# Routing inside the attention: the second stage of a transformer program is dissolved into the gaps of the first

## The reference, cut to what matters

```python
x = x + attention(layernorm(x)) @ Wo.T            # per head: softmax(q k^T * scale) v
h = layernorm(x)
logits = h @ gate_w.T                             # 14 experts
probs = softmax(logits)
top2_p, top2_i = top_k(probs, 2)
w = top2_p / max(top2_p.sum(-1), 1e-10)
x = x + clip(h + w0 * expert[top2_i[:, 0]](h) + w1 * expert[top2_i[:, 1]](h), -100, 100)
```

## Time and profile before

| | us |
|---|---|
| median of 3 runs | 2218.16 |
| lowest and highest | 2213.41, 2222.66 |
| the profiled execution | 2228.09 |
| its span, first to last instruction | 2226.4 |
| TensorE busy | 1696.7 (76%) |
| VectorE busy | 1467.5 (66%) |
| ScalarE busy | 1210.6 (54%) |
| GpSimd busy | 1360.6 (61%) |

### The profile page before, as it was taken

How to read it: one execution, slowest core, us unless ns; L and a number is a source line. 1 busy time by engine, 2 the same in 40 slices (tenths; PEclk the granted TensorE clock), 3 DMA queues, 4 the chain that set the end, 5 groups by cost and what they waited for, 6 DMA issues and landing times. The chain is left out here.

```text
span 2226.4 us, 59455 instructions
## 1 busy us (share of the span) xinstructions
PE 1696.7 (76%) x18769; PEld 1117.8 (50%) x18769; DVE 1467.5 (66%) x3940; ACT 1210.6 (54%) x2321; POOL 1360.6 (61%) x1087
## 2 busy tenths in 40 slices
PE   7978999999999999975442699377777766100997
PEld 3424656565566666645342588344444443000897
DVE  5756888888888888836444444178888887620453
ACT  4626888888888888854332355224444444021343
POOL 0005878787878887845446233488888883155465
PEclk9978999999999999985655799689999898555999
DMA  4753222222222222212221333400000000132332
GB/s 153 247 171 119 60 71 62 70 63 70 64 68 66 67 67 65 71 59 78 72 87 58 104 127 123 151 22 20 19 19 19 19 19 1 43 111 80 99 102 62
DMA packets 158123, 169.71 MB, mean 76 GB/s; under 512 B 39522, under 2 KB 124393, under 8 KB 157961
## 3 DMA queue, kind: packets, MB, share of 16 engines
q1 hardware_dynamic: 143128, 137.02, 20.1%
q0 software_dynamic: 13824, 29.43, 4.2%
q10 hardware_dynamic: 1008, 0.92, 0.1%
HBM read 93.57 MB, written 73.97 MB: 75 GB/s over the span
## 5 line engine op out<-in xcount | busy, mean ns | idle before, releaser
L769 DVE TENSOR_REDUCE halfmax<-p_m 128x1 f32<-128x512 f32 x1024 | 644.3, 681 | 125.8 <-PE p_m L638 123.1
L756 ACT ACTIVATE probs<-p_s,ESCALE 128x512 f32<-128x512 f32 x1024 | 643.9, 685 | 27.4 <-PE p_s L668 10.5
L638 PE MATMUL p_m<-ka,qa 96*32 96x512 f16 x4096 | 518.8, 390 | 12.8 <-DMA vh<-v 12.0
L668 PE MATMUL p_s<-qa,ka 98*32 98x512 f16 x4096 | 503.6, 383 | 8.8 <-DMA qa<-max_lo 6.4
L591 POOL TENSOR_TENSOR sum_p<-sum_p,probs 128x1024 f32<-128x1024 f32 x192 | 456.1, 2375 | 11.0
L675 PE MATMUL p_o<-probs,vh 128*32 128x256 f32 x4096 | 401.1, 380 | 0.3 <-ACT probs L756 0.3
L591 POOL TENSOR_TENSOR sum_p<-probs 128x1024 f32<-128x1024 f32 x64 | 152.2, 2378 | 165.8 <-ACT probs L756 165.8
L638 PEld LDWEIGHTS p_m<-ka,qa 96*32 96x32 f16 x4096 | 180.0, 97 | 125.0 <-DVE halfmax L769 19.4
L668 PEld LDWEIGHTS p_s<-qa,ka 98*32 98x32 f16 x4096 | 178.6, 96 | 122.1 <-ACT probs L756 12.4
L1652 PE MATMUL ln_p_cum<-ln_kv,c_tri 128*128 128x512 f32 (+1 forms) x384 | 166.5, 577 | 88.6 <-POOL ln_kv L1596 88.6
L1309 ACT ACTIVATE e_h<-e_p_h,e_w 128x256 f32<-128x256 f32 x316 | 126.1, 473 | 158.8 <-PE e_p_h L1288 84.8
(11 more groups left out here) (299 smaller groups left out, 2797.4 us busy)
## 6 DMA issues: line engine op xcount, KB each, us to landing
e_xb<-xs SPq DMA_DIRECT2D x40, 257.0 KB
e_xb<-xs SPq DMA_DIRECT2D x78, 128.0 KB, 2.0
ys<-e_y SPq DMA_DIRECT2D x78, 128.0 KB, 1.9
v<-pj_v SPq DMA_DIRECT2D x8, 1024.0 KB, 5.0
qa<-q SPq DMA_DIRECT2D x64, 128.0 KB, 2.7
ka<-k SPq DMA_DIRECT2D x64, 128.0 KB, 2.7
vh<-v SPq DMA_DIRECT2D x64, 128.0 KB, 2.2
o<-ot SPq DMA_DIRECT2D x64, 128.0 KB
```

Source lines behind the costliest of these rows:

```text
L638: mm = nc.tensor.matmul(max_bank(s, n)[j * DH0:(j + 1) * DH0, :], qa[s][0:KA, (n // 2) * P + j * DH0:(n // 2) * P + (j + 1) * DH0], ka[s][ ...
L668: mm = nc.tensor.matmul(score_bank(s, k, h)[j * DH0:(j + 1) * DH0, :], ka[s][:, cols], qa[s][:, q], start=True, stop=True, tile_position=( ...
L756: nc.scalar.activation(probs[k][:, h * HALF:(h + 1) * HALF], score_bank(s, k, h)[:, :], ACT.Exp, scale=ESCALE[:, 0:1]).then_inc(probs_d, 1)
L769: nc.vector.reduce_max(halfmax[s % 2][:, n // 2, n % 2:n % 2 + 1], max_bank(s, n)[:, :], AX.X).then_inc(max_read, 1)
```

## The change

`route2` is gone. Its work goes by whole sequences (8 tiles of 128 tokens) into `attend`, in "gaps": gap u is the place in TensorE's text around the denominators of unit u, and the place in VectorE's text behind the fourth maxima half, where the maxima are split. A sequence takes fifteen gaps from gap 12 + 8b on: 0 and 1 project, 1 and 2 add and take moments, 3 scales, 4 and 5 normalise and turn, 5 and 6 logits, 7 exponentials and the best two, 8 their indices, 11 counting and ranks, 12 places, 13 gates, and from 14 on GpSimd issues two scatters in each unit. Several sequences are under way at once. What belongs to gaps past 63 is done after the last unit, in the same block.

With it come: one PSUM bank for routing (`p_r`), taken from the maxima, which keep two of three; `TURN` 4 instead of 5, so that the maxima are turned just ahead of the denominators; the loops over units written out on all engines; the normalised rows kept in DRAM (`xn0`) instead of SBUF and read back to XN at the start of `e0`; zero rows written early in the attention; gate weights loaded before the experts' weights.

```diff
-TURN = 5
+TURN = 4
-MAX_BANKS = tuple(i % 3 for i in range(SLOTS * RING))
+MAX_BANKS = tuple(i % 2 for i in range(SLOTS * RING))
...
-        p_m = [ctx.enter_context(nc.psum_tensor(f"p_m{i}", [P, HALF], F32)) for i in range(3)]
+        p_m = [ctx.enter_context(nc.psum_tensor(f"p_m{i}", [P, HALF], F32)) for i in range(2)]
...
+        ST, NX, FIRST = KT, 3, 12
+        p_r = ctx.enter_context(nc.psum_tensor("p_r", [P, HALF], F32))
...
+        def sequence(gap, piece):
+            b, rest = divmod(gap - FIRST - piece, H0)
+            return b if rest == 0 and 0 <= b < B else None
...
         def _(sp):
...
+            load(SLOTS)
+            sp.wait_ge(zeros_d, 1)
+            zero_surplus(sp, xs, lambda n: zeros[:, :, :], E0, surplus_of(2, E0), surplus_out)
+            for u in range(UNITS):
+                if u + 2 < UNITS:
+                    rows_of_maxima(u + 2)
+                if u >= 1:
+                    spread_inverses(u - 1)
+                outputs_of = sequence(u, -1)
+                if outputs_of is not None:
+                    load_outputs(outputs_of)
+                if u >= 3:
+                    store(u - 3)
+                rows_of = sequence(u, 6)
+                if rows_of is not None:
+                    keep_rows(rows_of)
...
         def _(pool):
...
+            def scatter(h, half):
+                b = next((m for m in range(B) if 0 <= h - FIRST - 14 - m * H0 < H0), None)
+                if b is None:
+                    return
+                n = 2 * (h - FIRST - 14 - b * H0) + half
+                i, t, k = n // 8, n // 2 % G, n % 2
+                apart(pool, slot_d, b + 1, passed)
+                pool.indirect_dma_start(xs[:, :], bass.IndirectOffsetOnAxis(ap=slot[b % NX][:, n:n + 1], axis=0),
+                                        xn[b % NX][i][:, t, :], None).then_inc(rows_out[b % NX], 16)
...
+                    if n == 1 and u >= 3:
+                        normalise(u - 3)
+                    if n >= 2:
+                        scatter(u, n - 2)
...
         def _(pe):
...
+            def ranks(b):
+                pe.wait_ge(shift_d, 2 * b + 2)
+                if b + 1 < B - 1:
+                    pe.wait_ge(x_d, 2 * b + 4)
+                pe.wait_ge(hot_d, b + 1)
+                pe.wait_ge(seen_d, (b + 1) * ST)
+                nc.tensor.matmul(pos_ps, c["stri"][:, :], both[:, :, :], start=True, stop=False)
+                nc.tensor.matmul(pos_ps, c["ones"][:, :], seen[:, 0:ST, :], start=False, stop=True).then_inc(pos_d, 1)
...
             for u in range(UNITS):
-                rest_of_head(pe, u // SLOTS, u % SLOTS)
+                for k in range(2, KT):
+                    key_tile(u, k)
+                if u < LAST:
+                    for k in range(2):
+                        key_tile(u + 1, k)
+                if u + 2 < UNITS:
+                    max_turn(u + 2)
+                in_front(u)
+                denominators(u)
+                behind(u)
+            turn(B - 2, 0)
+            logits(B - 2, 0)
+            turn(B - 2, 1)
+            logits(B - 2, 1)
+            ranks(B - 2)
+            for i in range(2):
+                attention(B - 1, i)
+            for i in range(2):
+                turn(B - 1, i)
+                logits(B - 1, i)
+            ranks(B - 1)
...
         def _(act):
...
+                    if k == 4:
+                        b = sequence(u, 4)
+                        if b is not None:
+                            roots(b)
+                        if u:
+                            keep_outputs(u - 1)
...
         def _(dve):
...
+            def count_tiles(b):
+                dve.wait_ge(hot_d, b + 1)
+                from_first(dve, now_d, b)
+                from_first(dve, pos_d, b)
+                nc.vector.tensor_copy(seen[:, 0, :], seen[:, ST, :]).then_inc(seen_d, 1)
+                for t in range(ST - 1):
+                    dve.wait_ge(seen_d, b * ST + t + 1)
+                    nc.vector.tensor_tensor(seen[:, t + 1, :], seen[:, t, :], both[:, t, :], ALU.add).then_inc(seen_d, 1)
...
+            def segment(u):
+                if u + 1 < UNITS:
+                    row_maxima(u + 1)
+                for n in range(SCORES):
+                    if n == TURN:
+                        if u + 1 < UNITS:
+                            split_maxima(u + 1)
+                        if u >= 2:
+                            invert(u - 2)
+                        route(u - 1)
+                    if u + 2 < UNITS:
+                        half_max(u + 2, n)
...
-def route2(nc, c, X, XN, GATE, SLOT, tabs, o0, xs, wo, wg, oT):
...
+                for n in range(B):
+                    rows = slice(n * T, (n + 1) * T)
+                    sp.dma_start(kept[0][:, rows], kept[1][:, rows]).then_inc(kept_in, 16)
                 turned(sp, 0, 0, 0)
                 load(sp, AHEAD, 0, 1)
```

More of the change, by code:

```diff
@@ new lines, in attend @@
+        xT = sb("r_xT", [P, GT])
+        top, total, prob = sb("r_top", [P, G]), sb("r_total", [P, ST]), sb("r_prob", [P, ST, E0])
+        best, at = sb("r_best", [P, ST, 8]), sb("r_at", [P, ST, 8], U32)
+        atf, slotf = sb("r_atf", [P, ST, 2]), sb("r_slotf", [P, ST, 2])
+        hot, both = sb("r_hot", [P, ST, 2, E0]), sb("r_both", [P, ST, E0])
+        seen = sb("r_seen", [P, ST + 1, E0])
+        now, start = sb("r_now", [P, E0]), sb("r_start", [P, E0])
+        place, placed = sb("r_place", [P, ST, E0]), sb("r_placed", [P, ST, 2, E0])
@@ new lines, in denominators, with key_tile @@
+            def denominators(u):
+                pe.wait_ge(sum_p_d, SP0 + (u + 1) * len(POOL_SUMS))
+                spread(u, 1, c["ones"][:, 0:DH0], sum_p[u % 2], False, False)
+                for k in range(len(POOL_SUMS) + 1, KT):
+                    last = spread(u, 1, c["ones"][:, 0:DH0], probs[k], False, k == KT - 1)
+                last.then_inc(den_d, 1)
+            def key_tile(u, k):
+                nxt = (u, k + 2) if k + 2 < KT else (u + 1, k + 2 - KT)
+                for h in range(2):
+                    if nxt[0] < UNITS:
+                        score(*nxt, h)
+                    if u + 2 < UNITS:
+                        max_half(u + 2, 2 * k + h)
+                values(u, k)
@@ new lines, in attention @@
+            def attention(b, i):
+                pe.wait_ge(oT_in[i], (b + 1) * 32)
+                if i:
+                    pe.wait_ge(x_d, 2 * b + 1)
+                else:
+                    from_first(pe, shift_d, 2 * b)
+                if b == B - 1:
+                    pe.wait_ge(pos_read, B - 1)
+                for t in range(G):
+                    for cc in range(2):
+                        mm = nc.tensor.matmul(y_ps[:, t, :], oT[i][:, cc, t * P:(t + 1) * P], wo[:, cc, :],
+                                              start=(cc == 0), stop=(cc == 1))
+                mm.then_inc(y_d, 1)
@@ new lines, in turn, with logits @@
+            def turn(b, i):
+                pe.wait_ge(xn_d, 2 * b + i + 1)
+                if i:
+                    pe.wait_ge(shift_d, 2 * b + 1)
+                else:
+                    pe.wait_ge(x_d, 2 * b + 2)
+                    from_first(pe, pos_read, b)
+                for t in range(G):
+                    mm = nc.tensor.transpose(p_r[:, t * P:(t + 1) * P], xn[b % NX][i][:, t, :], c["ident"][:, :])
+                mm.then_inc(pxT_d, 1)
+            def logits(b, i):
+                pe.wait_ge(xT_d, 2 * b + i + 1)
+                for t in range(G):
+                    mm = nc.tensor.matmul(gate_ps[:, t, :], xT[:, t * P:(t + 1) * P], wg[:, :], start=True, stop=True)
+                mm.then_inc(gate_d, 1)
@@ new lines, in behind @@
+            def behind(gap):
+                b = sequence(gap, 0)
+                if b == 0:
+                    pe.wait_ge(weights_in, (E0 + 4) * 16)
+                if b is not None:
+                    attention(b, 0)
+                b = sequence(gap, 1)
+                if b is not None:
+                    attention(b, 1)
+                b = sequence(gap, 4)
+                if b is not None:
+                    turn(b, 0)
+                b = sequence(gap, 5)
+                if b is not None:
+                    turn(b, 1)
+                b = sequence(gap, 11)
+                if b is not None:
+                    ranks(b)
@@ L785, in invert @@
-        def invert(dve, r, s):
-            u = r * SLOTS + s
-            dve.wait_ge(few_in, ONE + (u + 1) * 16)
-            nc.vector.reciprocal(few[s % 2][:, :], few[s % 2][:, :]).then_inc(inv_d, 1)
+                    behind_tile(u, k)
+            for b in range(B - 2, B):
+                roots(b)
+                for i in range(2):
+                    for t in range(G):
+                        normalise(b, i, t)
+                for i in range(2):
+                    copy_turned(b, i)
+                exponentials(b)
@@ L825, in _ @@
+            invert(LAST - 1)
+            end = LAST % 2
```

939 lines of the change are left out of this document (403 added, 536 removed).

## The result

| | before | changed |
|---|---|---|
| median of the runs | 2215.8 us (4 runs, 2212.7 to 2222.7) | 2237.0 us (4 runs, 2233.2 to 2254.1) |
| ratio, with 95% interval | | 1.0102 [1.0054, 1.0150] |
| profiled execution | 2228.1 us | 2234.0 us |

The change made the kernel slower, by 1.0% on this chip. The forecast was 2192 us, 1% faster. Case B of the rivals had put 2239.

The account below looks back on a forecast made before the run. TensorE was taken to bound the attention (738.68 of 740 us busy), while routing hid nothing. -176 + 49 + 57 + 13 + 15 + 11 + 5 = -26 from 2228.1 gave 2202, less 9.9 for the median 2192 us; range 2125 to 2250.

Parts of the forecast that it names:

- Case B: Rival, attention: GpSimd's additions also hold up VectorE's operations of one SBUF input; VectorE's term 104, time 2239 us; chance 0.18.
- stage removed, with its tail: Routing between attention and experts: 262 us removed, a tail of 86 (78 to 105) left; saves 176 us.
- matmuls of TensorE: Attention: projections 25, turns 8, logits 13, ranks 3 added on full TensorE; together 49 us, nothing hides it.
- banks and turn: Attention: two banks for the maxima instead of three cost 15 us (0 to 38); the turn's new place nothing.
- start: Start of attention: first maxima bound by VectorE 3 us, zero DMAs ahead of unit 2's maxima rows 8; together 11.
- pauses of VectorE and ScalarE: Gaps of the attention: VectorE 57 us (31 for pauses, 26 for the counting chain), ScalarE 13 for normalising and table loads.
- experts and later: Start of the experts: normalised rows read back in eight DMAs, TensorE may wait; 5 us (0 to 12).
- One is much worse: Gap with the counting: eight dependent two-SBUF-input additions may each wait for GpSimd's; 5.2 us times five sequences, 26.
- 2.1 us each, 0.7 more than is free: Attention: VectorE's routing work over seven gaps per sequence; 44 such pauses cost 31 us.
- I take nothing: Attention: 76 of 128 scatters on GpSimd, 2.5 of 2.2 us spare per unit, within its slack; cost 0.
- Turning the maxima ahead of the denominators ... I take it as nothing: Attention: the turn's new place costs nothing, since the denominators cover the chain to the small DMAs.
- 49 and 30: Attention: bounds of the term for TensorE's added matmuls; 30 if VectorE's pauses fall into the same time.

Follow-up runs that it names:

- short sums: Changed kernel with GpSimd's additions of tiles cut to 32 of 1024 columns (denominators wrong): 2149.3 us, 0.9935 of the kernel before.
- chip B: One of three later chips; the changed kernel, run again there unaltered against the kernel before: 2199.2 against 2162.0 us, ratio 1.0168.

## Why the prediction was wrong

In the order of its sum, in us of the profiled executions on the first chip. Unnamed measured numbers are from its two profiles.

| step | predicted | measured |
|---|---|---|
| stage removed, with its tail | -176 | -171 (tail 91 instead of 86) |
| matmuls of TensorE | +49 | 56 busy |
| banks and turn | +15 | +18, of it 1 at the start (no routing, turn ahead) |
| start | +11 | 10, of it that 1 |
| pauses of VectorE and ScalarE | +57 and +13 | 167 - 56 - 28 = 83 together |
| experts and later | +5 | +10 (7 in the experts) |
| **sum** | **-26** | **+6** |

The pauses are what is left of the attention's growth when the matmuls are put in with their busy time. The run with the projections twice showed that matmuls are partly hidden, so the line between these two terms is drawn by reckoning, not by a run.

The largest single miss in the profile is the pauses' term, 83 instead of 70, and its parts were wrong in both directions. The chips of the other kind let it be taken apart. There the attention grew by 147.5 us. The kernel with short sums takes the waits for GpSimd away: its attention is 82.0 us longer than that of the kernel with banks and turn alone (991.3), and of it some 9 lie in the start (third period 25.5 against 16.1) and 56 in the matmuls. So pauses without waits cost some 17 us, where the prediction had 31 + 13 besides the chain. The waits for GpSimd cost 47 us, where the prediction had 26 for the chain and nothing for the rest. Together that is 64, close to 70, and the closeness is luck: two errors of opposite sign. On the first chip come the 19 us by which the attention grew more there, nearly all behind the first scatter.

The step of the mechanism that failed is therefore "One is much worse": the prediction charged GpSimd's additions to the counting chain alone, though seven other lines of the same gaps have two SBUF inputs, and it spoke of them as "2.1 us each, 0.7 more than is free". The earlier trace rows said what happens to any of them. Of the 71 us of excess 20 lie on the counting, 43 on these seven lines. Taking the counting's waits away shortened the attention by 22.5 us of the 47, so some 25 were left on lines that the prediction had at nothing (up to 8 of them moved there from the counting, to `r_shift`).

That step alone did not turn the sign, since the pauses without waits were put too high by about as much. The second step that failed is the one on the scatters in the attention, "I take nothing": it held on chip B, but on the first chip the units behind the first scatter are longer, some 17 us together. That the scatters are the cause is not shown. The rest of the miss in the sum is in sizes: matmuls 7, tail 5, experts 5, banks and start 2.

Case B came near in number, 2239 against 2237, and in part in kind. Its terms for the pauses, 104 and 13, were 34 too high, and the other terms (19) and the offset below (13) made up for it. Its condition, one SBUF input and a constant, is shown: the maximum with a constant (L1046) lasts 0.65 us instead of 0.17, and the copy `r_seen` (0.16 us alone) 1.26 to 1.80. But the copies, casts and operations with a constant hold only 13 of the 71 us of excess; most lies on two SBUF inputs outside the chain, which neither case had priced. Reductions, reciprocals and MAX8 of one SBUF input never waited.

The chain itself came out at its price by another way than the one described: not each addition waits. Two or three instructions of nine do, since TensorE's standing still stops GpSimd. But behind the chain come the ranks and 1.82 us until the next maxima half is there. The unit costs 8.4 us more than 12.75; of it 5.5 go with short sums (21.1 against 15.6), where the prediction had 5.2. The restart was left out.

The prediction cited the Trainium skill ("SBUF — State Buffer", section "SBUF: two separate sides") for two SBUF inputs and concluded that pauses of one input would not be lengthened. That was read too narrowly: the same rule names VectorE's two-port performance modes too, and the section says that an f32 copy from SBUF to SBUF takes one. The copies and casts of one SBUF input here waited as well (1.63 us in the median for 14 columns). It fits that the same copy with its output in PSUM took 148 ns.

"Turning the maxima ahead of the denominators ... I take it as nothing" failed as well, and was hidden by an opposite error: the bank alone costs 0.79 us a unit, over three times the 0.24 predicted, and the turn gives 0.47 back. Together they came out near the forecast by luck.

TensorE's term was small by 7 us: a projection took 2.05 us between other matmuls (28.7 / 14), not 1.79, though a second one behind it added only 1.78. Its bound "49 and 30" did not hold it. The tail's 79 us to the end of the tables were met by luck: the last sequence had its slots 61 us behind the last product instead of 54, and the tables took 18 us behind them instead of 25. On chip B the two are 49 and 18. What ended the tail was the queue of scatters, which the prediction had as "beside the tables".

The step from the profile to the median is another miss. The prediction took 9.9 us off, because the profiled execution of before lay that far above its median. The changed kernel's lay 3 us below its own. That is 13 us of the miss of 45, and 32 come from the sum. The chips add to this. Of the 262 us of the stage some 60 are waits that two of the later chips did not show at all, and on one of these, chip B, the change was slower by 1.7% rather than 1.0%. A forecast from one profile could not know that.

What stays open: what the event is that ends these waits, and whether the same cause makes the units slower behind the first scatter on such chips. Both come with scatters; a kernel without scatters in the attention was not tried. Open too is what of the 10 us behind the tail is the reading back of the rows: it was not moved by itself. How the gain of the counts in PSUM splits between the copy and the additions was not tried either.

## What to carry to other kernels

Before small work is moved under another engine's long additions, list each of its instructions with what it reads and writes: two SBUF inputs, or a copy or cast from SBUF to SBUF, can wait for whole additions of GpSimd, and an operand in PSUM freed it here. That difference was 47 us of attention on a chip where the whole change cost 37. A stage that is full on one engine has idle time in the others only as long as nothing in it waits for them; price a gap by the restart behind it too, and take a bank away only together with a reordering that pays for at least a part of it (here 0.47 of 0.79 us a unit).

## What the runs showed of the hardware

- A small instruction of VectorE waits behind a GpSimd addition as long as a large one: 14 columns lasted up to 2.33 us (0.17 alone), 224 columns up to 2.51 (0.39 alone).
- The same addition of 128x14 takes 180 ns with one operand and the output in PSUM and 174 with all in SBUF when nothing else runs, so PSUM costs 6 ns and saves up to 2.1 us.
- The median of the kernel before was 2162, 2165, 2216 and 2233 us on the four chips. Of the 71 us between the first and the last, 64 lie between the last product and the first load of expert rows (262 against 198 us in the profiles), nearly all in waits while scatters run.
- With scatters in the attention a unit of the same work took 13.89 us on two chips and 14.6 to 15.1 on the other two, with the same excess of VectorE.
